# Pacing GpSimd's gathers and scatters by the node loop in the first stage of a graph network

## The chip, the cores and the metric

The kernel runs on one core of a Trainium2 chip. The metric is the device time of one execution in microseconds; the median of three runs is given.

## The reference, cut to what matters

A network of four graph layers over 12500 nodes (64 features) and 200000 edges that are sorted by destination: typed attention, gated attention, a polynomial sum, and a convolution of three layers. Only the start of the first layer concerns us here:

```
h = jnp.maximum(_layernorm(x, axis=-1), 0.0)
...
k = typed_linear(x, Wk, ntype).reshape(n, h_heads, hs)
q = typed_linear(x, Wq, ntype).reshape(n, h_heads, hs)
v = typed_linear(x, Wv, ntype).reshape(n, h_heads, hs)
ke, qe, ve = (k[src], q[dst], v[src])
kw = typed_head_linear(ke, rel_att, etype)
qw = typed_head_linear(qe, rel_att, etype)
```

For every node the keys, values and query are made from the weights of its type. The kernel makes a table of keys and values for each node and each of the 8 edge types, and puts each query at the place of the node's first edge, so that the edge stage can read it in order. For that it must find where each node's edges start in the sorted destinations.

## The kernel before, in words

The nodes stand as 98 tiles of 128 (`T = 98`). The function `first_phase` (from L278) is the first stage; after it `graph_layers` (L2273) runs the edge stages and convolutions, whose gathers GpSimd issues one column of 128 rows at a time.

In the first stage the engines work so, each in the order written out:

- **The node loop** takes pairs of tiles (49), four pairs to a group (`GROUP = 8` tiles, `PER = 4`, `FULL = 12` groups and a tail of one pair). VectorE masks a group's normed features by node type (L759, semaphore `s_hm`), into one buffer, so a group's masking waits until all pairs of the group before are turned. TensorE turns a pair (L595, increments `s_tr`), ScalarE copies it (L523), TensorE projects keys, values and queries (L607, L612, increments `s_kv`), ScalarE copies them (L529, and the query by L530, which increments `s_q`), TensorE multiplies by the relations of the edge types (L623, `s_tab`), ScalarE copies the result in four pieces (L540, `s_tca`), and SP stores it to the table (L422). Of the buffers for the table there are two, so a table copy waits for the store of two pairs before (L537).
- **The norm** is done in two parts: of the first 16 tiles at once, of the other 82 beside the loop. The square root of the second part (L516) stands in ScalarE's order in the second group, between its second and third pair; VectorE then ends the norm (L749 to L751) and masks the third group.
- **Zeros.** The query buffer in memory has a row for every edge, and is filled with zeros before the queries are scattered. The zeros come from a buffer that VectorE clears (L698). The fill is cut into 64 pieces, sent two to a transfer: 16 pieces before the loop (L416 to L417, `AHEAD`), then two with each pair's table store in the first six groups (L425, `FILLED`). All are issued by SP.
- **The search.** TensorE and VectorE find for each node the segment of 32 destinations in which its edges start; GpSimd gathers the 99 columns of segments (L467 to L470, `s_win`), each an indirect DMA, back to back. When all have landed, VectorE counts within the segments and makes the starts (L805 to L824), after the masking of group 5 (`MIDDLE = 6`).
- **The scatters.** GpSimd waits for the starts and for all zeros (L471 to L472) and scatters the queries, one tile per indirect DMA (L473 to L481). Tile t waits until `t // 2 + 1` pairs of queries are copied. Before tile 64 it reads the end table (L474 to L478), which SP stores after its eighth group.

The loops of SP, ScalarE, TensorE and VectorE over the groups are device loops (`Fori`) with registers, but for a first and a last group or two. The lines that set GpSimd's pace are

```
            pool.wait_ge(s_dst, 16)
            pool.wait_ge(s_seg, 1)
            for t in range(T1):
                pool.indirect_dma_start(out=window[:, t, :], out_offset=None, in_=g.dst_tab,
...
            pool.wait_ge(s_start, 2)
            pool.wait_ge(s_zero, 16 * (9 + BLANKS // 2))
            for t in range(T):
...
                pool.wait_ge(s_q, t // 2 + 1)
                pool.indirect_dma_start(out=g.q_start, out_offset=bass.IndirectOffsetOnAxis(ap=g.start_i[:, t:t + 1].bitcast(U32), axis=0),
```

Of the kernel before, what the change touches and what calls it, by code (L numbers as in the profile page):

```python
# [277 lines left out]
def first_phase(nc, ctx, g, a):  # L278


    sem = lambda n: new_sem(nc, ctx, "fp_" + n)
# [10 lines left out]
    s_lkd = pool_sem(g, "looked")  # L292
    s_scat = pool_sem(g, "scattered")
    s_st = [sem("stored0"), sem("stored1")]
    GROUP = 8
    TWOS = T // 2
    PER = GROUP // 2
    FULL = T // GROUP
# [2 lines left out]
    T1 = T + 1  # L301
    TEN = 10
    RUNS = [range(t, min(t + TEN, T1)) for t in range(0, T1, TEN)]
    MIDDLE = FULL // 2
    EARLY = 2 * GROUP
    BLANKS = D
    AHEAD = 16
    FILLED = (BLANKS - AHEAD) // GROUP
    assert AHEAD + FILLED * GROUP == BLANKS and FILLED < MIDDLE + 2
    S1 = SEGS + 1  # L310
    at = 0
    q, at = view(g, at, T, D)
# [57 lines left out]
    with ExitStack() as inner:  # L370
# [10 lines left out]
        @block.sync  # L381
        def _(sp):
            def load(out, in_, signal, slow=False):
                sp.dma_start(out, in_, allow_slow_non_contiguous=slow).then_inc(signal, 16)

            def edges_in(buf, flat, signal):
                load(buf[0:EVEN, :], rows_of(flat, 0, EVEN), signal)
                load(buf[EVEN:P - 1, :], rows_of(flat, EVEN, P - 1), signal)
                load(buf[last, 0:LAST], flat[(P - 1) * J:E].rearrange("(a j) -> a j", a=1), signal)

            sp.wait_ge(s_pad, 1)
            edges_in(dst, a["dst"], s_din)
            sp.wait_ge(s_pad, 3)
            for p0, p1 in ((0, EVEN), (EVEN, P - 1)):
                load(g.X[p0:p1, :, :], a["x"][p0 * T:p1 * T, :].rearrange("(p t) f -> p t f", t=T), s_xin)
                load(ty[p0:p1, :], a["node_type_4"][p0 * T:p1 * T].rearrange("(p t) -> p t", t=T), s_xin)
            load(g.X[last, 0:REST, :], a["x"][(P - 1) * T:N, :].rearrange("(a t) f -> a t f", a=1), s_xin)
            load(ty[last, 0:REST], a["node_type_4"][(P - 1) * T:N].rearrange("(a t) -> a t", a=1), s_xin)
            sp.wait_ge(s_din, 16 * 3)
            sp.dma_start(g.dst_tab.rearrange("(p s) k -> p (s k)", p=P), dst_all).then_inc(s_dst, 16)  # L400
            sp.wait_ge(s_pad, 4)
            load(prev[1:P, :], a["dst"][0:(P - 1) * J].rearrange("(p j) -> p j", j=J)[:, J - 1:J], s_ein, slow=True)
            for buf, flat in ((src, a["src"]), (idx8, a["edge_type_8"]),
                              (g.pre[:, :], a["edge_weight1"].rearrange("e one -> (e one)"))):
                edges_in(buf, flat, s_ein)

            sp.wait_ge(s_pad, 5)
            sp.dma_start(g.s_start[0:EP, :].rearrange("(p j) a -> p (j a)", p=P), zeros).then_inc(s_zero, 16)
            for rows, width in ((g.rows0, R0), (g.rows1, R1), (g.rows3, R3), (g.rows3b, D)):
                sp.dma_start(rows[EP:EP + P, :], zeros[:, 0:width]).then_inc(s_zero, 16)  # L410
                sp.dma_start(rows[EP + P:EP + P + 1, :], zeros[0:1, 0:width]).then_inc(s_zero, 16)

            def blank(piece):
                sp.dma_start(blanks[:, piece, :], zeros.unsqueeze(1).to_broadcast([P, 2, J])).then_inc(s_zero, 16)

            for n in range(0, AHEAD, 2):  # L416
                blank(slice(n, n + 2))  # L417

            def body(i, n, filling=False):
                for x in range(n // 2):  # L420
                    wait(sp, s_tca, i * PER + (x + 1))
                    sp.dma_start(tab[sl(i, GROUP, 2 * x, 2), :, :].rearrange("a p n -> p a n"),  # L422
                                 tb[x % 2].rearrange("p a e c -> p a (e c)")).then_inc(s_st[x % 2], 16)
                    if filling:
                        blank(sl(i, GROUP, AHEAD + 2 * x, 2))  # L425
                wait(sp, s_q, i * PER + n // 2)
                sp.dma_start(q_tab[:, sl(i, GROUP, 0, n), :], q[:, sl(i, GROUP, 0, n), :]).then_inc(s_qdone, 16)

            body(0, GROUP, filling=True)
            with sp.Fori(1, FILLED) as i:  # L430
                body(i, GROUP, filling=True)
            with sp.Fori(FILLED, MIDDLE + 2) as i:
                body(i, GROUP)
            for k in range(3):
                wk = a[f"L3_gnn_W{k + 1}"]
                load(g.Wz[0:D, k, :], wk[0:D, :], s_wconv)
                load(g.Wt[0:D, k, :], wk[D:2 * D, :], s_wconv)
                to = g.Wz if k else g.Wt
                load(to[D:D + ED, k, :], wk[2 * D:2 * D + ED, :], s_wconv)
                load(to[D + ED:K17, k, :], a[f"L3_gnn_b{k + 1}"].rearrange("(a f) -> a f", a=1), s_wconv)  # L440
            wait(sp, s_start, 2)
            sp.dma_start(g.end_tab.rearrange("(p t) a -> p (t a)", t=T), g.end_i[:, :]).then_inc(s_look, 16)
            with sp.Fori(MIDDLE + 2, FULL) as i:
                body(i, GROUP)
            body(FULL, TAIL)
            wait(sp, s_look, 16)
            wait(sp, s_wconv, 16 * 12)
            wait(sp, s_qdone, 16 * (FULL + 1))
            for b in range(2):
                wait(sp, s_st[b], 16 * ((TWOS + 1 - b) // 2))  # L450

        @block.gpsimd
        def _(pool):
# [8 lines left out]
            pool.wait_ge(s_const, 6)  # L462
            pool.affine_select(out=dm, in_=g.ident[:, :], compare_op=ALU.not_equal, fill=-1.0,
                               base=1, pattern=[[-1, P]], channel_multiplier=1).then_inc(s_const, 1)
            pool.wait_ge(s_dst, 16)
            pool.wait_ge(s_seg, 1)
            for t in range(T1):  # L467
                pool.indirect_dma_start(out=window[:, t, :], out_offset=None, in_=g.dst_tab,
                                        in_offset=bass.IndirectOffsetOnAxis(ap=seg_i[:, t:t + 1].bitcast(U32), axis=0))\
                    .then_inc(s_win, 16)  # L470
# [3 lines that stand above are left out]
                if t == GROUP * (MIDDLE + 2):  # L474
                    pool.wait_ge(s_look, 16)
                    pool.indirect_dma_start(out=look, out_offset=None, in_=g.end_tab,
                                            in_offset=bass.IndirectOffsetOnAxis(ap=g.first[:, 0:1].bitcast(U32), axis=0))\
                        .then_inc(s_lkd, 16)  # L478
                pool.wait_ge(s_q, t // 2 + 1)
                pool.indirect_dma_start(out=g.q_start, out_offset=bass.IndirectOffsetOnAxis(ap=g.start_i[:, t:t + 1].bitcast(U32), axis=0),  # L480
                                        in_=q[:, t, :], in_offset=None).then_inc(s_scat, 16)  # L481
            pool.wait_ge(s_scat, 16 * T)
# [2 lines left out]
        def _(act):  # L485
# [57 lines left out]
            def body(i, n, left=TWOS):  # L543
                for x in range(n // 2):
                    if x == 2 and isinstance(i, int) and i == 1:
                        root(1, slice(EARLY, T))
                    if x + 2 < left:
                        copy_turned(i, x + 2)
                    if x + 1 < left:
                        copy_kv(i, x + 1)  # L550
                    copy_tab(i, x)
# [1 line left out]
            copy_turned(0, 0)  # L553
            copy_turned(0, 1)
            copy_kv(0, 0)
            body(0, GROUP)
            body(1, GROUP)
            with act.Fori(2, FULL - 1) as i:
                body(i, GROUP)
            body(FULL - 1, GROUP, left=TWOS - (FULL - 1) * PER)  # L560
            body(FULL, TAIL, left=TWOS - FULL * PER)
# [2 lines left out]
        def _(pe):  # L564
# [62 lines left out]
            def body(i, n, left=TWOS):  # L627
                for x in range(n // 2):
                    if x + 2 < left:
                        turn(i, x + 2)  # L630
                    if x + 1 < left:
                        project(i, x + 1)
                    if isinstance(i, int) and i == 0 and x == 0:
                        pe.wait_ge(s_wrel, 1)
                        pe.wait_ge(s_less, len(RUNS))
                    relate(i, x)
# [1 line left out]
            turn(0, 0)  # L638
            turn(0, 1)
            project(0, 0)  # L640
            body(0, GROUP)
            with pe.Fori(1, FULL - 1) as i:
                body(i, GROUP)
            body(FULL - 1, GROUP, left=TWOS - (FULL - 1) * PER)
            body(FULL, TAIL, left=TWOS - FULL * PER)
# [11 lines left out]
        def _(dve):  # L657
# [37 lines left out]
                v.tensor_scalar(steps[:, c * PART:c * PART + PART], iota_h, limits[:, c:c + 1], None, ALU.is_gt)  # L695
            dve.wait_ge(s_diff, 1)
            v.tensor_copy(delta.rearrange("p k s -> p (k s)"), ps_s[:, 0:2 * S1]).then_inc(s_oh, 1)
            v.memset(zeros, 0.0).then_inc(s_pad, 1)  # L698

            def count_less(n):  # L700
                ts = RUNS[n]
# [97 lines left out]
            dve.wait_ge(s_all, 3)  # L799
            v.tensor_scalar(g.allT[:, :], g.allT[:, :], f[:, 7:8], None, ALU.add).then_inc(s_all, 1)  # L800

            with dve.Fori(3, MIDDLE) as i:
                body(i, GROUP)

            dve.wait_ge(s_win, 16 * T1)  # L805
# [17 lines left out]
            v.tensor_tensor(g.start_i[:, :], start, node[:, 0:T], ALU.add).then_inc(s_start, 1)  # L823
            v.tensor_scalar(g.end_i[:, :], ends, float(EP), None, ALU.add).then_inc(s_start, 1)  # L824

            with dve.Fori(MIDDLE, FULL) as i:
                body(i, GROUP)
            body(FULL, TAIL)

# [1492 lines left out]
```

## Time and profile before

| | us |
|---|---|
| median of three runs | 11907.97 (11905.48 to 11908.42) |
| span of the profiled execution | 13242.4 |
| time of the profiled execution outside its span | not shown |
| begin of the second stage in the profile | 505.26 |
| GpSimd busy in the span | 9106.3 (69%) |
| VectorE, ScalarE, TensorE busy | 4015.6, 3476.7, 1352.0 |

The profile is of one execution with the hardware profiler on, 11.2% longer than the runs. Its views are the page (span, busy shares, chain, costliest groups), a table of busy times by stretch, a timeline (start, duration, engine, line, what is written and read, and in brackets the idle time of the engine before the instruction and what ended it), and waits. "remote" is a release by an increment that no instruction's record accounts for at that time; "issue" is idle time in which nothing shown was waited for. The ends of TensorE's records are modelled.

### The profile page before, as it was taken

The numbers are of one execution on the slowest core, as the hardware profiler recorded it, in microseconds if no ns is written. First come the engines' busy times: TensorE is split into PE (matmuls) and PEld (weight loads), VectorE is DVE, ScalarE is ACT, GpSimd is POOL, SyncE is SP. The second block draws the span as 40 slices with busy tenths as digits, with TensorE's granted clock in tenths as the row PEclk, the third lists the DMA queues.
The fourth block names the chain that finished last, engine by engine and source line by source line (L and its number), as shares of the span: only waits on it lengthen the run. The fifth ranks groups of instructions, "written<-read, shape, count | busy, mean of one in ns | idle before, by whom it ended". The sixth has DMA issues, their size and how long they took to land. (4 is left out here: it accounts for less than half of the span.)

```text
span 13242.4 us, 37433 instructions
## 1 busy us (share of the span) xinstructions
PE 1352.0 (10%) x6735; PEld 1005.3 (8%) x6735; DVE 4015.6 (30%) x5472; ACT 3476.7 (26%) x4561; POOL 9106.3 (69%) x8728
## 2 busy tenths in 40 slices
PE   5200000020000000395000000200000000000000
PEld 3100000010000000273000000200000000000000
DVE  2255555544445544695111111011111101111110
ACT  2333223312222222375232222122211212221121
POOL 3677777767777776402777777577777767777776
PEclk7655555555555555697555555555555555555555
DMA  7333333313333333001222222111111111111111
GB/s 277 133 97 97 98 95 95 100 34 90 98 95 94 94 99 81 14 1 32 61 58 61 58 58 60 40 50 46 49 46 46 49 39 50 46 49 46 46 49 42
DMA packets 404823, 919.05 MB, mean 69 GB/s; under 512 B 171046, under 2 KB 195277, under 8 KB 389496
## 3 DMA queue, kind: packets, MB, share of 16 engines
q0 software_dynamic: 278944, 386.91, 13.3%
q1 hardware_dynamic: 121832, 529.42, 10.9%
q14 instruction: 175, 1.43, 0.0%
q10 hardware_dynamic: 3824, 0.50, 0.0%
q8 instruction: 48, 0.79, 0.0%
HBM read 456.45 MB, written 459.77 MB: 69 GB/s over the span
## 5 line engine op out<-in xcount | busy, mean ns | idle before, releaser
L864 POOL DMA_INDIRECT arena<-tab,src x6256 | 6549.8, 1047 | 2894.4 <-issue 2101.0
L2244 DVE TENSOR_TENSOR_SCAN arena<-cv_keep,arena 128x768 f32<-128x768 f32 (+1 forms) x476 | 752.0, 1627 | 5757.2 <-issue 4526.3
L864 POOL DMA_INDIRECT arena<-tab,spread x1564 | 1644.1, 1051 | 518.5 <-issue 518.5
L2106 ACT COPY arena<-arena 128x1472 f32<-128x1472 f32 x204 | 545.3, 2673 | 3003.9 <-DMA arena<-tab,src 3003.9
L2111 ACT COPY arena<-arena 128x1472 f32<-128x1472 f32 (+1 forms) x204 | 588.3, 2884 | 551.8 <-DVE arena L2244 431.2
L1089 PE MATMUL e_t<-ident,arena 128*68 128x128 f32 (+1 forms) x2 | 0.8, 397 | 4433.5 <-PEq L1433 2223.3
L2168 PE MATMUL cv_t<-ident,arena 128*81 128x128 f32 (+1 forms) x294 | 137.9, 469 | 2917.7 <-ACT arena L2118 1528.3
L2105 ACT COPY arena<-arena 128x368 f32<-128x368 f32 x68 | 55.3, 813 | 1353.7 <-issue 1325.1
L2182 PE MATMUL cv_t<-ident,arena 128*64 128x128 f32 (+1 forms) x3 | 1.3, 425 | 3391.1 <-ACT arena L2111 3391.1
L951 ACT ACTIVATE ae_prob<-arena 128x92 f32<-128x92 f32 x68 | 17.1, 251 | 1228.8 <-remote 1152.7
L1089 PEld LDWEIGHTS e_t<-ident,arena 128*68 128x68 f32 (+1 forms) x2 | 0.3, 134 | 4433.9 <-issue 4433.9
L1502 DVE TENSOR_TENSOR arena<-arena,ge_small 128x23 f32<-128x23 f32 x68 | 13.3, 195 | 1064.8 <-DMA arena<-tab,src 1064.8
L1883 DVE TENSOR_SCALAR arena<-arena 128x448 bf16<-128x448 f16 x1252 | 324.8, 330 | 37.4 <-PE po_u L1766 20.4
L1766 PE MATMUL po_u<-arena,Hn 128*128 128x448 bf16 x1564 | 300.6, 354 | 291.4 <-DVE Hn L1873 291.4
L1025 DVE TENSOR_TENSOR arena<-arena,ae_prob 128x1472 f32<-128x1472 f32 x68 | 260.1, 3824 | 220.3 <-issue 217.2
L1465 ACT ACTIVATE ge_decay<-arena 128x768 f32<-128x768 f32 x68 | 56.4, 830 | 1015.4 <-issue 944.1
L992 DVE TENSOR_TENSOR_SCAN ae_work<-ae_keep,arena 128x768 f32<-128x768 f32 x136 | 240.1, 1765 | 224.2 <-remote 146.5
L1766 PE MATMUL po_u<-arena 128*128 128x448 bf16 x1564 | 298.9, 352 | 1.0 <-DVE arena L1883 1.0
L943 ACT ACTIVATE ae_work<-arena 128x768 f32<-128x768 f32 x136 | 208.5, 1533 | 300.7 <-DVE arena L1037 287.5
L2168 PEld LDWEIGHTS cv_t<-ident,arena 128*81 128x81 f32 (+1 forms) x294 | 53.9, 184 | 2953.8 <-ACT arena L2118 1538.3
L1034 DVE TENSOR_TENSOR_SCAN arena<-ae_work,arena 128x768 f32<-128x768 f32 x136 | 238.9, 1757 | 115.3 <-ACT ae_work L943 103.4
L1506 DVE TENSOR_TENSOR arena<-arena,ge_small 128x1472 f32<-128x1472 f32 x68 | 258.7, 3805 | 0.2 <-issue 0.2
(370 smaller groups left out, 6943.0 us busy)
## 6 DMA issues: line engine op xcount, KB each, us to landing
rows<-arena SPq DMA_DIRECT2D x68, 1506.5 KB
arena<-tab,src POOLq DMA_INDIRECT x6256
rows3b<-arena SPq DMA_DIRECT2D x136, 736.0 KB
rows<-arena SPq DMA_DIRECT2D x68, 920.0 KB
rows<-arena SPq DMA_DIRECT2D x68, 828.0 KB
tab<-arena SPq DMA_DIRECT2D x49, 1024.0 KB
q_start<-arena SPq DMA_DIRECT2D x32, 1564.0 KB
arena<-q_start SPq DMA_DIRECT2D x68, 736.0 KB
```

The lines of the kernel that those rows point to most:

```text
L864: pool.indirect_dma_start(out=rows[b][:, j, :], out_offset=None, in_=table, in_offset=bass.IndirectOffsetOnAxis(ap=idx[:, at:at + 1].bitca ...
L943: return nc.scalar.activation(works.rearrange("p (h d) j -> p h d j", h=HH), args[:, 0, :, h0:h0 + HH].rearrange("p j h -> p h j").unsquee ...
L992: v.tensor_tensor_scan(out=work[:, :], data0=keep[:, :], data1=qts[:, x * HF * C1:(x + 1) * HF * C1], initial=0.0, op0=ALU.mult, op1=ALU.a ...
L1025: v.tensor_tensor(mix[:, :, 1:C1].rearrange("p (h d) j -> p j h d", h=H), kv[:, :, D:2 * D].rearrange("p j (h d) -> p j h d", h=H), prob.u ...
L1034: ins = v.tensor_tensor_scan(out=part, data0=work[:, :], data1=part, initial=0.0, op0=ALU.mult, op1=ALU.add)
L1506: v.tensor_tensor(peak[:, :, 1:C1].rearrange("p f j -> p j f"), r[:, :, D:2 * D], pre.unsqueeze(2).to_broadcast([P, C, D]), ALU.mult).then ...
L1766: ins = nc.tensor.matmul(ps_u[:, x, 0:half], wide[c % 2][:, x * P:x * P + P, j], ring[:, n % RING, :], start=(n == 0), stop=(n == J - 1))
L1883: v.tensor_scalar(ring[:, n % RING, :], iota_hi, hi[:, n:n + 1], None, ALU.is_equal).then_inc(s_hot, 1)
L2106: nc.scalar.copy(chain[:, 0:D, 1:C1], rin[b].rearrange("p j f -> p f j")).then_inc(s_in, 1)
L2111: nc.scalar.copy(rows.rearrange("p j f -> p f j"), chain[:, :, 1:C1]).then_inc(s_copied, 1)
L2168: nc.tensor.transpose(ps_t[b][0:K_Z, 0:P], hd[b][:, 0:K_Z], g.ident[:, :]).then_inc(s_tr, 1)
L2244: ins = v.tensor_tensor_scan(out=part, data0=keep[:, 0:(f1 - f0) * C1], data1=part, initial=0.0, op0=ALU.mult, op1=ALU.add)
```

## The change

GpSimd's gathers of the search go free up to tile 32; from tile 33 on each third one waits until one more pair is turned. The scatter of tile t waits until `28 + t // 3` pairs of queries are copied (at most 49), or for `t // 2 + 1` as before where that is more. VectorE makes the starts after seven groups instead of six (`MIDDLE = 7`); SP's store of the end table stays after its eighth group, and the lookup goes from tile 64 to tile 72. GpSimd clears the zeros, with a semaphore of its own. 24 pieces of zeros precede the node loop, and five groups carry the other 40. The loops over groups are unrolled on all four engines.

```
+    s_blank = sem("zeros_made")
...
-    MIDDLE = FULL // 2
+    MIDDLE = FULL // 2 + 1
+    FREE = 33
     EARLY = 2 * GROUP
     BLANKS = D
-    AHEAD = 16
+    AHEAD = 24
     FILLED = (BLANKS - AHEAD) // GROUP
...
-            sp.wait_ge(s_pad, 5)
+            sp.wait_ge(s_blank, 1)
...
-            body(0, GROUP, filling=True)
-            with sp.Fori(1, FILLED) as i:
-                body(i, GROUP, filling=True)
-            with sp.Fori(FILLED, MIDDLE + 2) as i:
-                body(i, GROUP)
+            for i in range(MIDDLE + 1):
+                body(i, GROUP, filling=i < FILLED)
...
-            with sp.Fori(MIDDLE + 2, FULL) as i:
+            for i in range(MIDDLE + 1, FULL):
                 body(i, GROUP)
...
+            pool.memset(zeros, 0.0).then_inc(s_blank, 1)
             pool.wait_ge(s_dst, 16)
             pool.wait_ge(s_seg, 1)
             for t in range(T1):
+                if t >= FREE and (t - FREE) % 3 == 0:
+                    pool.wait_ge(s_tr, (t - FREE) // 3 + 1)
...
-                pool.wait_ge(s_q, t // 2 + 1)
+                pool.wait_ge(s_q, max(t // 2 + 1, min(MIDDLE * PER + t // 3, TWOS)))
...
-            body(0, GROUP)
-            body(1, GROUP)
-            with act.Fori(2, FULL - 1) as i:
+            for i in range(FULL - 1):
                 body(i, GROUP)
...
-            body(0, GROUP)
-            with pe.Fori(1, FULL - 1) as i:
+            for i in range(FULL - 1):
                 body(i, GROUP)
...
-            v.memset(zeros, 0.0).then_inc(s_pad, 1)
...
-            with dve.Fori(3, MIDDLE) as i:
+            for i in range(3, MIDDLE):
                 body(i, GROUP)
...
-            with dve.Fori(MIDDLE, FULL) as i:
+            for i in range(MIDDLE, FULL):
                 body(i, GROUP)
```

## Rows read from the trace of the kernel before

**Rows 1.** The head of the page.
```profile
span 13242.4 us, 37433 instructions
```

**Rows 2.** Timeline, end of the first stage: start, duration, engine, line, operands, idle before.
```profile
460.62 0.97 POOL L480 DMA_INDIRECT q_start<-arena,start_i  x1 [1.98 <-ACT arena L530]
461.67 2.05 ACT L540 COPY arena<-fp_tab 128x512 f32<-128x512 f32 x4 [1.33 <-PE fp_tab L623]
461.89 0.97 POOL L480 DMA_INDIRECT q_start<-arena,start_i  x1 [0.30 <-issue]
...
465.90 2.06 ACT L540 COPY arena<-fp_tab 128x512 f32<-128x512 f32 x4 [1.23 <-PE fp_tab L623]
...
491.21 0.97 POOL L480 DMA_INDIRECT q_start<-arena,start_i  x1 [0.30 <-issue]
...
495.61 2.05 ACT L540 COPY arena<-fp_tab 128x512 f32<-128x512 f32 x4 [2.17 <-PE fp_tab L623]
...
505.26 7.36 SPq L925 DMA_DIRECT2D arena<-q_start  x2
```

**Rows 3.** Stretches of the first stage: us, busy us and instructions by engine, clock, DMA share, GB/s.
```profile
140.00:190.00 50.00, 3.13 (x15) 3.14 (x16) 11.85 (x6) 3.35 (x8) 21.47 (x23) 0.50 0.19 61
...
240.00:300.00 60.00, 45.00 (x246) 30.26 (x246) 13.49 (x15) 27.11 (x63) 0.00 (x0) 0.84 1.01 409
```

**Rows 4.** Timeline, 85 to 187 us: ScalarE, TensorE, VectorE and one gather.
```profile
85.96 0.94 POOL L468 DMA_INDIRECT arena<-dst_tab,arena  x1 [0.30 <-issue]
...
91.74 0.63 ACT L523 COPY arena<-fp_turn 128x512 f32<-128x512 f32 x1
...
95.34 1.00 PE L612 MATMUL fp_kv<-Wq,arena 128*128 128x64 f32 x8
...
114.93 0.59 ACT L523 COPY arena<-fp_turn 128x512 f32<-128x512 f32 x1 [7.78 <-remote]
159.03 0.37 ACT L529 COPY arena<-fp_kv 128x256 f32<-128x256 f32 x1 [43.51 <-remote]
...
175.83 2.06 ACT L540 COPY arena<-fp_tab 128x512 f32<-128x512 f32 x4 [16.26 <-remote]
177.75 0.30 ACT L516 ACTIVATE small<-small 128x82 f32<-128x82 f32 x1
...
184.45 2.29 DVE L759 TENSOR_TENSOR arena<-Hn,types 128x2048 f32<-128x2048 f32 x1
```

**Rows 5.** All gathers of the search, by line: shortest, median, longest in ns, first and last start.
```profile
L468 POOL DMA_INDIRECT arena<-dst_tab,arena x99: 941/947/5473, 31.1 to 167.2; - x99
```

**Rows 6.** Timeline, first stretch of the scatters.
```profile
320.52 1.00 POOL L480 DMA_INDIRECT q_start<-arena,start_i  x1 [152.34 <-issue]
...
396.83 0.97 POOL L480 DMA_INDIRECT q_start<-arena,start_i  x1 [0.30 <-issue]
404.96 0.37 ACT L529 COPY arena<-fp_kv 128x256 f32<-128x256 f32 x1 [31.62 <-remote]
```

**Rows 7.** Timeline, the zeros' buffer and the first gather.
```profile
14.21 1.36 DVE L698 MEMSET arena<- 128x1564 f32 x1 [0.28 <-issue]
...
31.15 1.11 POOL L468 DMA_INDIRECT arena<-dst_tab,arena  x1 [27.49 <-DVE arena L719]
```

**Rows 8.** DMA issues of the first 1500 us: what, engine, count, KB each.
```profile
tab<-arena SPq DMA_DIRECT2D x49, 1024.0 KB
q_start<-arena SPq DMA_DIRECT2D x32, 1564.0 KB
```

**Rows 9.** Timeline, 73 to 80 us: a gather beside VectorE's subtraction.
```profile
73.55 5.63 DVE L735 TENSOR_TENSOR Hn<-X,small 128x5248 f32<-128x5248 f32 x1
...
74.52 5.47 POOL L468 DMA_INDIRECT arena<-dst_tab,arena  x1 [0.30 <-issue]
```

**Rows 10.** DMA queues from 80 to 90 us: packets, MB, share of 16 engines.
```profile
q8 instruction: 1, 0.02, 0.6%
```

**Rows 11.** Waits of GpSimd in the first 510 us: total, times, longest.
```profile
POOL arena L476 <- DMA end_tab<-end_i: 17.4, 1, 17.4
```

More of the change, by code:

```diff
@@ L303, in first_phase @@
     RUNS = [range(t, min(t + TEN, T1)) for t in range(0, T1, TEN)]
-    MIDDLE = FULL // 2
+    MIDDLE = FULL // 2 + 1
+    FREE = 33
     EARLY = 2 * GROUP
     BLANKS = D
-    AHEAD = 16
+    AHEAD = 24
     FILLED = (BLANKS - AHEAD) // GROUP
-    assert AHEAD + FILLED * GROUP == BLANKS and FILLED < MIDDLE + 2
+    assert AHEAD + FILLED * GROUP == BLANKS and FILLED < MIDDLE + 1
     S1 = SEGS + 1
```

## The prediction

> **What bounds the kernel now.** The head of the page gives the span, 13242.4 us [rows 1]; the three timed runs have a median of 11907.97 us, so the profiled execution is 11.2% longer than they are, and no time outside its span is shown. I make the sum in profiled microseconds and multiply the difference at the end by 11907.97/13242.4 = 0.899. The change touches only the first stage; the next one begins at 505.26 [rows 2]. Every microsecond by which this stage ends earlier is one less in total, because what follows begins with gathers that read its tables.
>
> I read the stages next. From 140 to 190 us TensorE and ScalarE are busy 3 us each of 50 and DMA 19%; from 240 to 300 TensorE is busy 45 us of 60 and DMA is full at 409 GB/s [rows 3]. So the stage is idle in its first part and full in its second. The timeline says why. The projection of 95.34 has its records end near 96.3, but ScalarE's copy that waits for its increment starts at 159.03, after 43.51 us put down to "remote", and the table copy after it at 175.83, after another 16.26 us [rows 4]. TensorE has done the work, and its increments arrive late. Meanwhile GpSimd issues gathers back to back: that of tile 33 starts at 85.96 [rows 4], the last, of tile 98, at 167.2 [rows 5], so one per 1.25 us, and 8 us after it everything moves. Behind that wait stands the square root of L516 (177.75), and behind that VectorE's masking of the third group (184.45) [rows 4], without which TensorE has no tile to turn.
>
> The same happens at the scatters. The first starts at 320.52, the 60th at 396.83 (1.29 us each), and a copy that follows a projection waits 31.62 us and starts at 404.96, once GpSimd has stopped for want of a query [rows 6]. Later two scatters go out per pair of tiles, and the pairs follow each other every 4.23 us (461.67 to 465.90) without such a wait [rows 2]. My reading: **GpSimd's unbroken run of indirect DMAs holds back TensorE's increments**; where the run has gaps they arrive at once. No row shows the path on which they are held.
>
> **The change part by part.**
>
> *Zeros on GpSimd.* The fill leaves VectorE (1.36 us at 14.21) for GpSimd, which idles 27.49 us before its first gather at 31.15 [rows 7]. That idle time covers it; without it some 1.4 us. SP comes to the zeros only after its loads. Nothing.
>
> *24 zero pieces ahead instead of 16.* A transfer carries two pieces, 1564 KB; a table store is 1024 KB [rows 8]. Four more transfers stand in SP's queue and in the DMA ring ahead of the first table store: 4 x 1.60 MB at 409 GB/s [rows 3] make it 15.7 us later. Table copies wait for the store two pairs back. The bytes are the same in all and DMA is idle soon after, so I cost this at nothing; if the square root came directly behind these stores it would be up to 15.7 us.
>
> *Gathers paced.* Tiles 0 to 32 go free, then three per turned pair. The seventh pair's copy starts at 91.74, the eighth's at 114.93 [rows 4]; tile 54 is the first that needs the eighth, and without a wait it would start at 85.96 + 21 x 1.25 = 112. Until then nothing differs. Then GpSimd stops, the eighth turn's increment arrives (by 114.93 at the latest), three more gathers go (3.75 us), and the increments behind it follow: projection and table copied by about 121 instead of 177.75, then the square root. From its start to the masking's end are 9.0 us (177.75 to 184.45 + 2.29) [rows 4]: 130 instead of 186.7, **57 us earlier**. Bounds: 67 us, if the increments come the moment GpSimd stops; 40, if the 15.7 us of zeros fall on this path. The other 42 gathers take 14 pairs; 3.75 us of the 6.7 that a pair takes there (below) is not the limit, and the windows are done before the eighth group's masking (MIDDLE is now 7), which needs the 28th turned pair.
>
> *Scatters start.* Before, 133.8 us pass from the masking's end to the first scatter (186.7 to 320.52), set by the landing of the last zero piece, which goes out with pair 23. Now it goes out with pair 19. ScalarE does 7 instructions per pair, and 63 in 60 us [rows 3], so a pair takes 6.7 us and four pairs 27 us. The zeros land at 130 + 133.8 - 27 = 237. But the first scatter now also waits for 28 query pairs: 7 pairs at 4.25 us after the last piece is issued, about 15 us before it lands (222): **252**, 68 us earlier than before. A start that was late is gone; what is late next is the node loop.
>
> *Scatters paced.* Scatter t waits for pair 28 + t//3, so 63 go beside 21 pairs, and 35 and the lookup are left when the loop is done. The period P of a pair beside three scatters is in no row. Low end: 4.25, as beside two scatters [rows 2]. High end: three scatters in series with that, 3 x 1.29 + 4.25 = 8.1. I take 5.0, near the low end, since bursts of two held nothing back, and half a microsecond of it for VectorE's hold on GpSimd: a gather took 5.47 us beside VectorE's 5.63 us subtraction [rows 9], and the five maskings left, of 2.29 us, can cost 11 us over 21 pairs. The Trainium skill, SBUF — State Buffer, section "SBUF: two separate sides", says that some VectorE operations lock GpSimd out of the port on which it writes descriptors; these two rows agree. By that rule the 11 us are certain, without it they are chance, and the sum moves by no more than that. So 252 + 21 x 5.0 = 357, and then 36 x 1.29 = **46 us of scatters with nothing beside them**. That is new: before, the last scatter (491.21) began ahead of the last table copy (495.61) [rows 2]. The last scatter ends at 403, takes some 2 us to land, and the 7.6 us that lay between the last copy's end (497.66) and the next stage stay: 412 instead of 505.
>
> *Loops unrolled.* More code is fetched: one packet of instructions took 0.6% of 16 engines over 10 us, 0.96 us [rows 10]. With some 14 more (an estimate: ten groups of about 250 instructions of TensorE, one packet each, and a few for the rest) at most 13 us if each is waited for, and a gain of a few us if the loops' register work is on the path. I take nothing. The lookup goes from tile 64 to 72; its wait of 17.4 us for the end table [rows 11] goes, which stood beside waits for queries: nothing.
>
> **Sum:** 505 - 412 = 93 us; times 0.899, 84; 11908 - 84 = 11824 us. With P at 4.25 it is 109 us (11810), with the 67 us too 119 (11801); with P at 8.1 it is 28 us (11883).
>
> **The rivals.**
> 1. *The lateness is not there in the timed runs, or is not GpSimd's.* Before would then mask the third group at about 105, scatter from 239 and end its 98 scatters at 239 + 126 = 365. After: 15.7 us later for the zeros, hence a start at 242, then 105 and 46: 393. **28 us slower, 25 in the runs: 11933.** The mechanism is the tail that the pacing leaves; it decides once P exceeds 3.7 in this case, and 9.4 in the forecast's. For it: the only evidence is an execution that is 11% slower than the runs. Against it: two stalls that begin and end with GpSimd's runs. The same section of the Trainium skill (SBUF — State Buffer) has TensorE wait on nobody for SBUF, by which GpSimd could not be the cause there and this rival would hold; no row here shows whether SBUF is where the increments are held. Chance 0.15.
> 2. *The increments stay late in bursts of three.* P is then 8 or more, which leaves 28 us; with the early part half as good, nothing: 11905. For it: three scatters are 3.87 of 4.25 us, almost unbroken. Against it: the wait itself breaks the run, since GpSimd can't go on until an increment comes. Chance 0.15.
> 3. *The forecast*, 0.70.
>
> **How the numbers follow.** A difference under 0.2% (24 us) can't be told from none here. The forecast is 11824, its own range 11800 to 11885. The range for 8 in 10 goes from 11785 (both low bounds, and some gain of the loops' register work) through rival 2 to just short of rival 1's value, 11930. Faster 0.70, same 0.15, slower 0.15, from the three cases.
>
> **What would show it.** In the profile after, ScalarE's "remote" waits for projections shrink from 43.51 and 31.62 us to under 10; the masking of the third group ends near 130; the first scatter starts near 252; 35 scatters stand alone at the end of a stage that ends near 412. I am wrong if the masking moves but the loop beside the scatters takes over 8 us per pair (rival 2), or if the stage shortens in the profile and the time doesn't (rival 1).

## The result, and the profile after

The changed kernel takes 11924.54 us (median of 20 runs, 11921.64 to 11928.25), the kernel before 11907.02 (20 runs): 1.0015 of it, with an interval of 1.0009 to 1.0021. It is 17.5 us slower. I had forecast 84 us faster; the time lies within my range of 11785 to 11930, but near its slow end, and it moved the other way. Rival 1 had named 25 us slower.

The head of the page after, and the gathers and scatters by line (shortest, median and longest in ns, first and last start in us):

```profile
span 11921.9 us, 36940 instructions
```

```profile
L470 POOL DMA_INDIRECT arena<-dst_tab,arena x99: 938/945/5462, 31.1 to 213.6; - x99
```

```profile
L482 POOL DMA_INDIRECT q_start<-arena,start_i x98: 964/969/2279, 255.2 to 393.9; - x98
```

Look at the span first. It agrees with the runs to 0.03%, whereas the span before was 11.2% above them [rows 1]. The execution profiled before the prediction was unlike the timed runs, so its stage can't be held against this one. The first experiment gives a stage that can.

The timeline after, at the places of [rows 2] and [rows 4] (start, duration, engine, line, operands, idle before):

```profile
48.78 1.00 PE L612 MATMUL fp_kv<-Wq,arena 128*128 128x64 f32 x8
...
49.49 0.94 POOL L470 DMA_INDIRECT arena<-dst_tab,arena  x1 [0.30 <-issue]
49.72 1.99 PE L623 MATMUL fp_tab<-Wrel,arena 64*128 64x512 f32 x8
49.83 0.37 ACT L531 COPY arena<-fp_kv 128x256 f32<-128x256 f32 x1 [1.21 <-PE fp_kv L612]
...
92.77 2.05 ACT L542 COPY arena<-fp_tab 128x512 f32<-128x512 f32 x4 [33.79 <-DMA tab<-arena]
...
115.83 0.30 ACT L518 ACTIVATE small<-small 128x82 f32<-128x82 f32 x1
...
122.53 2.29 DVE L757 TENSOR_TENSOR arena<-Hn,types 128x2048 f32<-128x2048 f32 x1
...
255.17 1.00 POOL L482 DMA_INDIRECT q_start<-arena,start_i  x1 [40.61 <-ACT arena L532]
...
316.79 2.06 ACT L542 COPY arena<-fp_tab 128x512 f32<-128x512 f32 x4 [1.25 <-PE fp_tab L623]
...
321.02 2.06 ACT L542 COPY arena<-fp_tab 128x512 f32<-128x512 f32 x4 [1.25 <-PE fp_tab L623]
...
349.30 0.97 POOL L482 DMA_INDIRECT q_start<-arena,start_i  x1 [0.30 <-ACT arena L532]
...
393.89 0.97 POOL L482 DMA_INDIRECT q_start<-arena,start_i  x1 [0.30 <-issue]
407.26 7.02 SPq L923 DMA_DIRECT2D arena<-q_start  x2
```

The changed stage is almost the one I described: the third group is masked by 124.8 us (I said 130), the first scatter starts at 255.2 (252) and waits last for a query, and the stage ends at 407.3 (412). One pair beside three scatters takes 4.23 us (316.79 to 321.02). In the mean of the 21 pairs it is 4.48 us: the 63 scatters beside the loop go from 255.17 to 349.30. The profile has no "remote" wait at all. At 49.83, in the midst of gathers at one per 1.25 us, a copy starts 0.05 us after the end of the record of TensorE's projection (48.78 + 1.00).

### The profile page after: what moved, and what is told of

Its sections match the earlier page's. It is cut to its first block and busy times, and to the rows that moved or that the text cites. A ratio compares the mean times of both kernels' runs of the same rounds, so it can differ in the third digit from the quotient of the medians.

```text
span 11921.9 us, 36940 instructions
## 1 busy us (share of the span) xinstructions
PE 1345.2 (11%) x6735; PEld 1003.8 (8%) x6735; DVE 4006.8 (34%) x5471; ACT 3476.4 (29%) x4561; POOL 8309.3 (70%) x8729
## 5 line engine op out<-in xcount | busy, mean ns | idle before, releaser
L862 POOL DMA_INDIRECT arena<-tab,src x6256 | 5906.3, 944 | 2587.9 <-issue 2565.6
L862 POOL DMA_INDIRECT arena<-tab,spread x1564 | 1476.7, 944 | 476.5 <-issue 476.5
L949 ACT ACTIVATE ae_prob<-arena 128x92 f32<-128x92 f32 x68 | 17.1, 251 | 1008.2 <-DVE arena L1017 1008.2
```

The lines of the kernel that those rows point to most:

```text
L862: pool.indirect_dma_start(out=rows[b][:, j, :], out_offset=None, in_=table, in_offset=bass.IndirectOffsetOnAxis(ap=idx[:, at:at + 1].bitca ...
```

## The experiments

**The kernel before, unchanged, profiled again.** No edit.

> The kernel before, unchanged, profiled once more. Theory A (the late increments belong to that one profiled execution, whose span was 11% above the runs): span near 11907 us, no waits put down to remote in the first stage, the masking of the third group near 110 us, and the first stage ends near 390, some 17 us ahead of the changed kernel's 407. Theory B (GpSimd's unbroken run of indirect DMAs holds back TensorE's increments): again a span near 13240, again remote waits of 30 to 45 us, first stage near 505. Time in both: 11907.

Measured: 11905.03 us; 0.9999 of the kernel before (0.999 to 1.0009). Its head, its scatters, and its timeline where [rows 2, 4, 6] stood:

```profile
span 11904.5 us, 37433 instructions
```

```profile
L480 POOL DMA_INDIRECT q_start<-arena,start_i x98: 965/969/2781, 246.1 to 376.8; - x98
```

```profile
77.08 2.05 ACT L540 COPY arena<-fp_tab 128x512 f32<-128x512 f32 x4 [17.75 <-DMA tab<-arena]
...
99.34 0.30 ACT L516 ACTIVATE small<-small 128x82 f32<-128x82 f32 x1
...
100.37 5.62 DVE L751 SCALAR_TENSOR_TENSOR Hn<-Hn,small 128x5248 f32<-128x5248 f32 x1
101.22 5.59 POOL L468 DMA_INDIRECT arena<-dst_tab,arena  x1 [0.30 <-issue]
106.03 2.29 DVE L759 TENSOR_TENSOR arena<-Hn,types 128x2048 f32<-128x2048 f32 x1
...
111.06 1.81 PE L612 MATMUL fp_kv<-Wq,arena 128*128 128x64 f32 x8
...
112.90 0.37 ACT L529 COPY arena<-fp_kv 128x256 f32<-128x256 f32 x1 [2.72 <-PE fp_kv L612]
113.09 0.94 POOL L468 DMA_INDIRECT arena<-dst_tab,arena  x1 [0.31 <-issue]
...
116.63 2.05 ACT L540 COPY arena<-fp_tab 128x512 f32<-128x512 f32 x4 [3.19 <-PE fp_tab L623]
116.84 0.94 POOL L468 DMA_INDIRECT arena<-dst_tab,arena  x1 [0.31 <-issue]
...
274.77 2.29 DVE L759 TENSOR_TENSOR arena<-Hn,types 128x2048 f32 x1 [14.80 <-PE fp_turn L595]
275.12 2.78 POOL L480 DMA_INDIRECT q_start<-arena,start_i  x1 [0.30 <-issue]
...
376.81 0.97 POOL L480 DMA_INDIRECT q_start<-arena,start_i  x1 [0.30 <-issue]
390.13 7.33 SPq L925 DMA_DIRECT2D arena<-q_start  x2
```

Theory A holds. The same gathers go out back to back, again one per 1.25 us (three from 113.09 to 116.84), and no wait is put down to "remote". The copy of 112.90 starts 0.03 us after the end of TensorE's record (111.06 + 1.81). The square root is at 99.3 where the first profile had 177.75, the first scatter at 246.1 where it had 320.52, and the stage ends at 390.1, not 505. Against this, the change's stage ends 407.26 - 390.13 = 17.1 us later, which is the 17.5 us of the runs. About nine of them are a later first scatter (255.2 against 246.1), eight a longer run of scatters (138.7 us from first to last, against 130.7).

**Scatters free.**

```
-                pool.wait_ge(s_q, max(t // 2 + 1, min(MIDDLE * PER + t // 3, TWOS)))
+                pool.wait_ge(s_q, t // 2 + 1)
```

> The changed kernel with the scatters waiting only for their own pair of queries, as before. Theory A1 (the tail of scatters left after the node loop costs the time): the first scatter starts near 240 us, when the last zeros land, 98 at 1.275 us end near 365, the stage ends near 378 instead of 407, time near 11895, below the kernel before. Theory A2 (the four zero transfers ahead of the loop cost it) and A3 (the pacing of the gathers costs it): no change beyond 5 us, 11924. Theory B: the scatters hold back TensorE, the loop gets longer, the time rises above 11924.

Measured: 11896.80 us, 27.7 below the changed kernel; 0.9993 of the kernel before (0.9984 to 1.0002). The scatters, the first of them, and the end of the stage:

```profile
L482 POOL DMA_INDIRECT q_start<-arena,start_i x98: 965/969/2653, 235.8 to 367.8; - x98
```

```profile
235.80 1.00 POOL L482 DMA_INDIRECT q_start<-arena,start_i  x1 [22.19 <-DVE end_i L822]
...
381.17 7.19 SPq L923 DMA_DIRECT2D arena<-q_start  x2
```

A1 holds to 2 us in the time and 3 to 4 us in the stage. The scatters start 19 us sooner, because they don't wait for 28 queries but for the starts, which VectorE ends at 235.4, and need 132 us. The two kernels were measured in different sets of runs, each with runs of the kernel before: held against those, the changed kernel is 17.5 us above and this one 8.8 below. So the pacing of the scatters costs some 26 us here, and the rest of the change gives some of it back in the medians, though this interval just reaches 1.

**Gathers free.**

```
-                if t >= FREE and (t - FREE) % 3 == 0:
-                    pool.wait_ge(s_tr, (t - FREE) // 3 + 1)
```

> The changed kernel with all gathers of the search back to back. A3: the windows are done earlier, some 10 to 17 us less, 11907 to 11915. A1 and A2: the starts are made behind the masking of the seventh group in any case, no change beyond 5 us, 11924. Theory B: TensorE's increments come late between 112 and 160 us, the masking of the third group moves back by 30 us or more, the time rises by 20 us or more.

Measured: 11923.05 us; 1.0014 (1.0005 to 1.0023). No change beyond 5 us, so A3 falls. So does theory B once more: with 99 gathers back to back the square root comes at 117.2, against 115.8 with the pacing, and no wait is put down to "remote".

**Sixteen pieces ahead.**

```
-    AHEAD = 24
+    AHEAD = 16
```

> The changed kernel with 16 zero pieces ahead of the loop and six filling groups, as before. A2: the first table store comes 15.7 us sooner, and so does all behind it: 11908. A1: the square root comes some 15 us sooner, but four more pairs carry zeros at 2.45 us more each, so the 28th query comes only 5 us sooner: 11919. A3: no change.

Measured: 11915.86 us; 1.0009 (1.0 to 1.0018), 8.7 below the changed kernel (7.2 when each is held against the kernel before of its own set), between A1's 5 and A2's 16. The scatters, and the four-piece table copies of the loop, here and in the changed kernel (that one second):

```profile
L482 POOL DMA_INDIRECT q_start<-arena,start_i x98: 963/969/2286, 243.7 to 383.4; - x98
...
L542 ACT COPY arena<-fp_tab x196: 585/601/623, 51.3 to 345.8; 128x512 f32<-128x512 f32 x196
```

```profile
L542 ACT COPY arena<-fp_tab x196: 586/600/622, 51.8 to 356.3; 128x512 f32<-128x512 f32 x196
```

With the pacing the last scatter starts 37.6 us after the last table copy in both (383.4 - 345.8; 393.9 - 356.3), and in the kernel with free gathers too (393.6 - 356.0). The pacing ties the end of the stage to the node loop, and eight more pieces ahead lengthen the loop by 10.5 us.

**24 pieces ahead, alone.** The kernel before with

```
-    AHEAD = 16
+    AHEAD = 24
```

> The kernel before with 24 zero pieces ahead of the loop and five filling groups, nothing else. If the earlier zeros bring the start of the scatters from 246 to 236 us, as the changed kernel with free scatters shows, and the 98 scatters then run 131 us as before: stage end 380, time 11897. If it is the unrolled loops or the later making of the starts that gave those 10 us: 11907, no change.

Measured: 11895.93 us; 0.9993 (0.9984 to 1.0002), 8.9 below the kernel before in the medians, though the interval of the ratio just reaches 1. First scatter 233.6, last 366.2. Without the pacing the same eight pieces are a gain of 9 us in the medians: the starts are ready at 206.9, the first scatter waits for the zeros until 233.6, and the end follows from there. The view puts this wait down to "issue"; that it is the zeros follows from the order of the program, which waits there only for the starts, the zeros and the first query pair. And in all seven profiles in which the starts were ready well before, the first scatter comes 14.6 to 15.1 us after SP's last zero transfer starts.

**Loops unrolled, alone.** The kernel before with its device loops over groups written out, as in the change.

> The kernel before with the loops over groups unrolled on SP, ScalarE, TensorE and VectorE, nothing else. If the end is set by GpSimd and by the zeros, and code loading is covered: within 3 us of 11906. If the loops' register work or waits on registers delay the zeros' issue: 5 to 10 us less. If the fetching of the longer code stalls TensorE: 5 to 13 us more.

Measured: 11906.03 us; 1.0 (0.9991 to 1.0009). Nothing, as costed.

**Scatters paced, alone.** The kernel before with

```
-                pool.wait_ge(s_q, t // 2 + 1)
+                pool.wait_ge(s_q, max(t // 2 + 1, min(28 + t // 3, TWOS)))
```

> The kernel before with the scatter of tile t waiting for 28 + t//3 query pairs, nothing else. If the pacing's tail is the whole cost: the first scatter at about 254 us, 63 beside the loop until about 343, then 36 operations of 1.275 us, stage end 402, 12 us more than before: 11919. If the pacing costs only beside the later starts or the zeros of the changed kernel: within 3 us of 11906.

Measured: 11915.12 us; 1.0008 (0.9999 to 1.0017), 10.3 more in the medians, where 12 were expected. The interval just reaches 1. The first scatter waits for the zeros:

```profile
243.41 1.00 POOL L480 DMA_INDIRECT q_start<-arena,start_i  x1 [62.69 <-DMA q_start<-arena]
```

The last starts at 383.0, 36.9 after the last table copy. The stage ends at 396.3, 6.2 later than in the second profile of the kernel before. The other 4 us of the time are not accounted for; single executions of this kernel differ by 5 us (11912.33 to 11917.61). The 10.3 us are also what the changed kernel with 16 pieces lies above the kernel before of its set (11915.86 against 11905.57). So with 16 pieces the pacing of the scatters is, in the medians, the whole cost of the change; the 24 pieces, a gain of 9 us without it, are a loss of 7 beside it.

**Everything free, starts after six groups.** The changed kernel without both pacings and with `MIDDLE = FULL // 2`.

> The changed kernel with gathers and scatters free and the starts made after six groups, as before; the unrolled loops, the 24 pieces and the zeros on GpSimd stay. If the zeros set the start of the scatters: 236 us, stage end 381, time 11897, as with the scatters alone set free. If the starts (made behind the seventh group's masking, 233 us) set it there: up to 10 us earlier, down to 11888.

Measured: 11896.31 us; 0.9993 (0.9984 to 1.0002). First scatter 235.1, though the starts are ready at 206.7: the zeros are as late as the starts were in the version with free scatters, and there is no gain over it.

**More pieces ahead.** The kernel of the last experiment with `AHEAD = 32` and `AHEAD = 40`, and the kernel before with `AHEAD = 32` and no other edit.

> The changed kernel with gathers and scatters free, the starts after six groups, and 32 zero pieces ahead of the loop. If the zeros still set the start of the scatters: about 226 us, and 131 us for them would end at 357; but the loop gets 10 us longer once more (last query near 361), so the last scatters follow it: stage end near 377, time 11892, some 4 us under the version with 24 pieces. If the loop is then the bound with its whole length, or the starts are later than the zeros: no gain, 11896 or a little more.

> As the version with 32 pieces, with 40. If the loop is now the bound (its last query at 361 us already ends with the last scatter): the loop gets another 7 to 10 us longer, stage end 384 to 386, time 11898 to 11900. If the start of the scatters still counts: 11885.

> The kernel before with 32 zero pieces ahead of the loop, nothing else. If the number of pieces ahead is all that counts: 11890, as the version with unrolled loops, zeros on GpSimd and 32 pieces. If unrolling and the zeros on GpSimd have a share there: 11892 to 11896.

Measured: 11890.16 us, 0.9985 (0.9976 to 0.9994), with 32 pieces; 11900.44, 0.9996 (0.9987 to 1.0005), with 40; 11888.17, **0.9987 (0.9978 to 0.9996)**, for the kernel before with 32, which by one changed number is faster than both kernels. Held against the kernel before of their own sets, the two versions with 32 gain 16.5 and 16.4 us: the number of pieces ahead is all that counts, and the unrolled loops and the zeros on GpSimd have no share. The waits of table copies for their stores (total, times, longest) with 32 and with 40, and what the first scatter waited for with 40:

```profile
ACT arena L540 <- DMA tab<-arena: 109.5, 16, 52.4
```

```profile
ACT arena L540 <- DMA tab<-arena: 110.7, 11, 71.1
...
POOL q_start L480 <- DVE end_i L820: 61.9, 1, 61.9
```

The longest wait of a copy grows by 16 to 19 us with each eight pieces (17.7 with 16, 33.8 with 24, 52.4, 71.1), while their total hardly moves. With the starts made after six groups, the starts are ready at 193.1, 206.9, 224.9 and 236.3 us with 16, 24, 32 and 40 pieces, since they stand behind the delayed square root, and the first scatter comes at 246.1, 233.6, 225.1 and 236.5. So the zeros set it with 16 and 24, the starts with 32 and 40. With 32 the two meet: the last zero transfer starts at 209.80, and 14.6 to 15.1 us on from there is 224.4 to 224.9. With 40 I had expected the loop to be the bound; the time came out as said, but the trace shows another reason, so that hit is luck.

## Why the prediction was wrong

**The step that failed is the reading.** "GpSimd's unbroken run of indirect DMAs holds back TensorE's increments" was drawn from coincidence in a single profile. With the same run of gathers, neither the second profile of the kernel before nor the profile with free gathers in the changed kernel has such a wait. Every other profile of this study lies within about 0.1% of its kernel's median.

The first profile held signs against the reading that I passed over. In the midst of the same run (gathers start at 85.96 [rows 4], 87.21 and 88.46), a copy starts 0.04 us after the end of the projection's record:

```profile
86.86 1.00 PE L612 MATMUL fp_kv<-Wq,arena 128*128 128x64 f32 x8
...
87.90 0.37 ACT L529 COPY arena<-fp_kv 128x256 f32<-128x256 f32 x1 [0.65 <-PE fp_kv L612]
```

And its page is odd far beyond TensorE's increments. Two groups of the later stages, each in the first profile and then in the second (busy us, mean ns, idle before and what ended most of it):

```profile
L864 POOL DMA_INDIRECT arena<-tab,src x6256 | 6549.8, 1047 | 2894.4 <-issue 2101.0
L951 ACT ACTIVATE ae_prob<-arena 128x92 f32<-128x92 f32 x68 | 17.1, 251 | 1228.8 <-remote 1152.7
```

```profile
L864 POOL DMA_INDIRECT arena<-tab,src x6256 | 5905.9, 944 | 2588.2 <-issue 1905.6
L951 ACT ACTIVATE ae_prob<-arena 128x92 f32<-128x92 f32 x68 | 17.1, 251 | 1008.1 <-DVE arena L1019 1008.1
```

This one group of gathers accounts for 644 of the 1338 us by which the first span is longer, and a wait that the second profile puts down to VectorE is "remote" in the first. What disturbed that one execution stays open; nothing here reproduced it.

**The sum's side of before** took 505 us from that execution, where 390 is right. The factor 0.899 spread its excess evenly, but the excess was no scale: the gathers of the search are issued at 1.25 us in both profiles, and the 115 us of excess in the first stage came with the waits that I wanted to remove. So all that I had named as signs came true in the changed kernel, whose stage I had nearly right, and the time still moved the other way.

**Point by point.** Gathers paced, 57 us: there was nothing to gain; the root of the changed kernel comes 16.5 us later than before (115.8 against 99.3), which is the 15.7 us of the zeros that I had costed at nothing and kept as a bound, and now shown by the table copy's wait of 33.79 us, against 17.75 before. Scatters start, 68 us earlier: 9 us later. Scatters paced: P is 4.48 in the mean, near the low end of my bounds, and not 5.0. The 11 us that I allowed for VectorE's hold came to 4.8 us of longer scatters (2.14, 2.14, 2.28 and 2.14 us against 0.97), and the pairs beside them kept their 4.24 us. The 46 us of tail are there (349.30 to 394.9); they are the price of the change. That the stage ends so near my 412 is partly luck: P makes it 11 us earlier, while a later start and 12.4 us instead of 9.6 behind the last scatter make it 6 later. Zeros on GpSimd and unrolled loops: nothing, as said. 24 pieces ahead: I took nothing; alone they are worth 9 us in the medians, since they bring forward the landing of the last zero piece. I had used that very dependence for the start, but booked it under the scatters.

**Rival 1 was right** in mechanism and sign, and nearly in size. It said 239 and 365 for the first scatter and the end of the scatters before (246.1 and 377.8), 242 and 393 after (255.2 and 394.9). The size is partly luck: it had 3 us of later start and 25 of longer run, and measured are 9 and 8. I gave it 0.15, although I had written that all evidence came from an execution 11% slower than the runs. The statement of the Trainium skill, SBUF — State Buffer, "SBUF: two separate sides", that TensorE waits on nobody there, is not contradicted by any later profile. The part on VectorE and GpSimd agrees only in part. A gather of 5.59 us beside VectorE's 5.62 us and a scatter of 2.78 us beside a masking of 2.29 us in the second profile of the kernel before show the hold again. But the same section reports that `tensor_tensor` was not seen to stall a DMA, and the masking and the subtraction of [rows 9] are TENSOR_TENSOR; here the measurement decides.

## What to carry to other kernels

Compare the span of a profile with the timed runs before anything else: at 11% apart, a wait that it shows may not be in the runs, and a second profile is worth more than any argument on its cause. Here no single factor would have put that profile right. Where one engine issues a fixed run of transfers that ends the stage, ask only when it can start and what makes it pause; a pace that is tied to another loop puts its remainder behind that loop. Moving bulk transfers ahead is a gain as long as they are what the run waits for, and stops being one when they delay the work that prepares it.

## What the runs showed of the hardware that I had not expected

An execution under the profiler can differ from the timed ones by long waits for increments (43.51 us [rows 4]) and by slower gathers in a later stage (1047 ns in the mean, against 944), while the gathers of the search look regular (median 947 ns [rows 5], against 944). Beside the same unbroken run of gathers in the second profile of that kernel, ScalarE's waits for TensorE were 2.72 and 3.19 us. And zeros and table stores from one queue kept their order: each eight pieces put ahead (four transfers of 1564 KB) made the longest wait for a table store 16 to 19 us longer.
